# The first tiles of a two-layer convolution kernel: channel 0's Toeplitz tiles read from SBUF, and a reordered start

## The reference

```
h  = sin(freq * (z @ w1 + b1)); h = sin(freq * (h @ w2 + b2)); h = sin(freq * (h @ w3 + b3))
hx = (h @ wo) * decay                       # the same with the Y weights gives hy: [256, 64] each
y  = causal 2-d convolution of x with the outer product hx[:, c] * hy[:, c]     (done by FFT)
x1 = y + x * bias[c]

scores = x1 @ x1.T / 16                     # per image and channel, 256 x 256
x2  = x1 + sum(scores * weights[c], -1, keepdims)
out = (x2 - mean) * rsqrt(var + eps) * gamma[c] + beta[c]    # mean and var per channel
```

## Time and profile before

| | us |
|---|---|
| median of 3 runs | 950.36 (950.07 to 951.35) |
| the profiled execution | 953.63 |
| its span, first to last instruction | 950.9 |
| PE busy | 930.9 (98%) |
| DVE busy | 749.4 (79%) |
| ACT busy | 682.0 (72%) |
| POOL busy | 672.5 (71%) |

### The profile page before, as it was taken

How to read it: one execution, slowest core, us unless ns; L and a number is a source line. 1 busy time by engine, 2 the same in 40 slices (tenths; PEclk the granted TensorE clock), 3 DMA queues, 4 the chain that set the end, 5 groups by cost and what they waited for, 6 DMA issues and landing times.

```text
span 950.9 us, 18901 instructions
## 1 busy us (share of the span) xinstructions
PE 930.9 (98%) x5312; PEld 815.0 (86%) x5312; DVE 749.4 (79%) x2457; ACT 682.0 (72%) x1088; POOL 672.5 (71%) x520
## 2 busy tenths in 40 slices
PE   7999999999999999999999999999999999999994
PEld 5888888888888888888888888888888888888883
DVE  2677887887877888887887887887887878887886
ACT  2447777777677777777777778777777778777776
POOL 2676777776687777777777776776776776776752
PEclk9999999999999999999999999999999999999997
DMA  7767999997899999989798999979799999988954
GB/s 222 265 170 219 251 257 301 261 241 291 228 276 288 208 303 289 272 237 290 199 307 293 213 287 303 267 248 287 228 271 302 246 252 296 274 247 293 256 141 187
DMA packets 91439, 244.09 MB, mean 257 GB/s; under 512 B 17184, under 2 KB 42016, under 8 KB 83232
## 3 DMA queue, kind: packets, MB, share of 16 engines
q1 hardware_dynamic: 73568, 235.73, 85.0%
q10 hardware_dynamic: 17856, 8.20, 3.4%
HBM read 176.52 MB, written 67.37 MB: 256 GB/s over the span
## 4 chain that ended last, share of the span: by engine, by line
PE 78%; POOL 9%; issue 8%; DVE 2%; DMA 1%; ACT 1%; POOLq 0%; DVEq 0%
PE ps_c L525 30%; PE ps_u L525 26%; PE ps_z L525 22%; POOL zl L417 3%; POOL xl L397 3%; POOL toep L390 2%; POOL wl L405 1%; POOL rstd L378 1%; DVE z_sb L718 1%; DMA toep_whole<-filters_padded 1%; DVE ul L758 0%; ACT uh L464 0%; POOL stat L371 0%; DMA par<-params_in 0%; DVE products L731 0%
## 5 line engine op out<-in xcount | busy, mean ns | idle before, releaser
L417 POOL TENSOR_TENSOR zl<-z_sb,zh 128x1024 fp32r<-128x1024 f32 x127 | 304.1, 2395 | 241.1 <-ACT zh L510 241.1
L731 DVE CUSTOM_DVE_ANT_0 products<-z_sb,ps_c 128x256 bf16<-128x256 f32 x504 | 182.2, 418 | 147.7 <-PE ps_c L525 147.7
L485 ACT ACTIVATE out_sb<-z_sb,shift,gain 128x256 f32<-128x256 f32 x496 | 257.3, 591 | 21.1 <-DMA out<-out_sb 15.7
L525 PE MATMUL ps_z<-uh,toep 128*128 128x512 f32 x768 | 271.4, 408 | 0.2 <-DVE z_sb L718 0.2
L464 ACT ACTIVATE uh<-ps_u 128x1024 fp32r<-128x1024 f32 x127 | 130.5, 1028 | 165.9 <-PE ps_u L525 165.9
L525 PE MATMUL ps_u<-toep,xh 128*128 128x256 f32 x1016 | 235.1, 313 | 2.8 <-POOL toep L390 2.4
L525 PE MATMUL ps_c<-zh,wh 128*128 128x512 f32 x504 | 196.3, 390 | 1.3 <-POOL zl L417 1.2
L525 PE MATMUL ps_c<-zh,wl 128*128 128x512 f32 x504 | 196.1, 389 | 0.0
L525 PE MATMUL ps_c<-zl,wh 128*128 128x512 f32 x504 | 196.1, 389 | 0.0
L525 PE MATMUL ps_u<-toep_whole,xt_sb 128*128 128x128 f32 x1016 | 195.8, 274 | 0.0
L742 DVE BATCH_NORM_STATS2 stat<-z_sb 128x6 f32<-128x256 f32 x512 | 179.4, 413 | 0.1
(11 more groups left out here) (79 smaller groups left out, 913.7 us busy)
## 6 DMA issues: line engine op xcount, KB each, us to landing
xt_sb<-xt_in SPq DMA_DIRECT2D x64, 1024.0 KB, 10.8
x_sb<-x_in SPq DMA_DIRECT2D x128, 512.0 KB, 9.1
out<-out_sb SPq DMA_DIRECT2D x124, 512.0 KB, 7.5
w_sb<-wt_in SPq DMA_DIRECT2D x64, 256.0 KB, 7.8
toep_whole<-filters_padded SPq DMA_DIRECT2D x64, 256.0 KB, 7.8
everyone<-partition_moments ACTq DMA_DIRECT2D x62, 128.0 KB, 8.7
out<-z_sb SPq DMA_DIRECT2D x2, 512.0 KB, 3.1
out<-z_sb SPq DMA_DIRECT2D x4, 256.0 KB, 3.4
```

The source lines that it names most:

```text
L417: nc.gpsimd.tensor_tensor(low, z_sb[:, r, h], high.bitcast(F32), ALU.subtract)\
L485: last = nc.scalar.activation(to[:, k, b], z_sb[:, r, h, k, b], ACT.Identity, bias=shift[:, r, g:g + 1], scale=gain[:, r])
L525: return nc.tensor.matmul(o, a, b, start=start, stop=stop)
L731: last = nc.vector.tensor_tensor_reduce(products[:, cs.slot(2), k, b], z_sb[:, r, h, k, b], bank[:, k, b], 1.0 / math.sqrt(SIDE), 0.0, ALU ...
```

## The change

Seven edits, in the order of time:

1. In the filter's layers the argument of half 1 is computed by ACT straight from PSUM (an Identity activation with scale freq / 2 pi and bias `bias_turns`, a new 128 x 3 tile that DVE fills once) and no longer by DVE. DVE's order is now argument 0, turns 0, part 0, turns 1, part 1. The table of the sine is asked for by a dummy activation at the very start. `WARM_LAYER` goes from 3 to 2, `WARM_TOEPLITZ` from 28 to 14.
2. Channel 0's two Toeplitz parts no longer come from DRAM. Each is one DMA of 128 KB from one partition of `filt` in SBUF, 128 overlapping windows of 1 KB: part 1 (Y) first, then the store to DRAM, then part 0 (X). Channel 1 on still come from DRAM.
3. ACT and POOL split channel 0's parts one by one, each with a semaphore of its own for part 1.
4. PE's first product u(0) runs in two passes over its four places: the first without the low part of the tile, and the high times low products behind them, behind a wait for that low part. The first z then waits for part 0.
5. In the first five steps ACT rounds u at the head of the step and not after the x and w parts.
6. Channel 1's tile is split one step earlier, in front of xh of its own step, on ACT and POOL.
7. Statistics take two images at once: bn_stats over 512 numbers in which the two images' numbers alternate (it keeps even and odd numbers apart), so two instead of four per pair, and bn_aggr takes 24 numbers instead of 48.

```diff
-WARM_FIRST, WARM_LAYER, WARM_TOEPLITZ = 3, 3, 28
+WARM_FIRST, WARM_LAYER, WARM_TOEPLITZ = 3, 2, 14
...
+    def toeplitz_step(st):
+        if st.static() and 2 <= st.number() <= 3:
+            return st.trail(0 if st.number() == 2 else LAG_T + 1)
+        return st.trail(LAG_T)
...
+            def load_first_toeplitz(f, landed):
+                row = filt[f * CH:f * CH + 1, 1:1 + SIDE]
+                windows = bass.AP(row.tensor, row.offset, [row.ap[0], [1, P], [1, SIDE]])
+                sp.dma_start(toep_whole[:, 0, f, :], windows).then_inc(landed, 16)
...
             sp.wait_ge(filt_ready, 1)
+            load_first_toeplitz(1, first_s_landed)
             sp.dma_start(pad_dram[:, :, :].rearrange("f c n -> (f c) n"), filt[:, :])\
                 .then_inc(filt_stored, 16)
+            load_first_toeplitz(0, t_landed[0])
             sp.wait_ge(filt_stored, 16)
...
                 ts = st.trail(LAG_LOAD_T)
-                if starts(ts):
+                if starts(ts) and not first_channel(ts):
...
-                means = stat[:, r].rearrange("p g (h s) -> p g h s", h=2)[:, :, :, 1]
-                nc.gpsimd.tensor_tensor(means, means, red[:, r].unsqueeze(2).broadcast_to([P, GROUPS, 2]),
-                                        ALU.add).then_inc(shifted, 1)
+                means = stat[:, r].rearrange("p g (b s) -> p (g b) s", b=PAIR)[:, :, 1]
+                nc.gpsimd.tensor_tensor(means, means, red[:, r], ALU.add).then_inc(shifted, 1)
...
-                ts = st.trail(LAG_T)
-                if starts(ts):
+                def low_toeplitz(ts, parts):
                     t = ts.ring(2)
                     wait_chan(pool, th_ready, ts, 1)
-                    nc.gpsimd.tensor_tensor(toep[:, t, :, 1], toep_whole[:, ts.ring(XR)],
-                                            toep[:, t, :, 0].bitcast(F32), ALU.subtract)\
+                    nc.gpsimd.tensor_tensor(toep[:, t, parts, 1], toep_whole[:, ts.ring(XR), parts],
+                                            toep[:, t, parts, 0].bitcast(F32), ALU.subtract)\
                         .then_inc(tl_ready, 1)
+                ts = toeplitz_step(st)
+                if starts(ts):
+                    if first_channel(ts):
+                        pool.wait_ge(first_sh_ready, 1)
+                        nc.gpsimd.tensor_tensor(toep[:, 0, 1, 1], toep_whole[:, 0, 1],
+                                                toep[:, 0, 1, 0].bitcast(F32), ALU.subtract)\
+                            .then_inc(first_sl_ready, 1)
+                    else:
+                        low_toeplitz(ts, slice(0, 2))
                 if active(st):
...
+                if starts(ts) and first_channel(ts):
+                    low_toeplitz(ts, slice(0, 1))
...
+            act.wait_ge(const_ready, 4)
+            nc.scalar.activation(sine_loaded[:, :], minus_half[:, :], ACT.Sin)
             for layer in range(3):
+                act.wait_ge(layer_done, 2 * layer + 2)
+                if layer == 0:
+                    act.wait_ge(bias_turns_ready, 1)
+                nc.scalar.activation(arg[:, HALVES[1]], ps_u[:, 1, 0, 0:P], ACT.Identity,
+                                     bias=bias_turns[:, layer:layer + 1], scale=freq_turns[:, 0:1])\
+                    .then_inc(second_arg, 1)
                 for i, half in enumerate(HALVES):
-                    act.wait_ge(reduced, 6 * layer + 6 + i)
+                    act.wait_ge(reduced, 5 * layer + 4 + 2 * i)
                     nc.scalar.activation(hid[:, half], part[:, half], ACT.Sin, scale=TWO_PI_BELOW)\
                         .then_inc(hid_ready, 1)
+            def round_u(us):
+                if active(us):
+                    wait(act, u_done, us, 1)
+                    wait(act, y_done, us, -1)
+                    nc.scalar.activation(uh[:, us.slot(2)], u_bank(us)[:, :, :, :], ACT.Copy)\
+                        .then_inc(uh_ready, 1)
             def stage(st):
+                filling = st.static() and st.number() <= 4
+                if filling:
+                    round_u(st.trail(LAG_U))
+                def high_toeplitz(ts):
+                    r = ts.ring(XR)
+                    parts = slice(0, 2)
+                    if first_channel(ts):
+                        parts = slice(0, 1)
+                        act.wait_ge(first_s_landed, 16)
+                        nc.scalar.activation(toep[:, 0, 1, 0], toep_whole[:, 0, 1], ACT.Copy)\
+                            .then_inc(first_sh_ready, 1)
+                    act.wait_ge(t_landed[r], ts.turn(XR) * 16)
+                    wait(act, y_done, ts, -2)
+                    nc.scalar.activation(toep[:, ts.ring(2), parts, 0], toep_whole[:, r, parts], ACT.Copy)\
+                        .then_inc(th_ready, 1)
+                ts = toeplitz_step(st)
+                if starts(ts) and filling and ts.channel() == 1:
+                    high_toeplitz(ts)
...
+                if starts(ts) and not (filling and ts.channel() == 1):
+                    high_toeplitz(ts)
+                if not filling:
+                    round_u(st.trail(LAG_U))
...
+                if first_channel(zs):
+                    pe.wait_ge(tl_ready, 1)
...
                 us = st.trail(LAG_U)
                 if active(us):
                     r, t = us.ring(XR), us.ring(2)
-                    if us.first_of_channel():
+                    first = first_channel(us) and not second_pair(us)
+                    if first:
+                        pe.wait_ge(first_sh_ready, 1)
+                    elif us.first_of_channel():
                         wait_chan(pe, tl_ready, us, 1)
                     wait(pe, xl_ready, us, 1)
                     if not second_pair(us):
                         wait(pe, ul_ready, us, 0)
                     s = us.slot(4)
-                    for h in range(BLOCKS):
-                        rows = slice(P * h, P * (h + 1))
-                        for b in range(PAIR):
-                            o = u_bank(us)[:, h, b, :]
-                            mm(o, xh[:, s, b, rows], toep[:, t, 1, 0, :], True, False)
+                    places = [(h, b, slice(P * h, P * (h + 1))) for h in range(BLOCKS) for b in range(PAIR)]
+                    for h, b, rows in places:
+                        o = u_bank(us)[:, h, b, :]
+                        mm(o, xh[:, s, b, rows], toep[:, t, 1, 0, :], b == 0 or not first, False)
+                        if not first:
                             mm(o, xh[:, s, b, rows], toep[:, t, 1, 1, :], False, False)
-                            mm(o, xl[:, s, b, rows], toep[:, t, 1, 0, :], False, False)
-                            last = mm(o[:, P:SIDE], xt_sb[:, r, PAIR * us.half() + b, 1, rows],
-                                      toep_whole[:, r, 1, 0:P], False, True)
+                        mm(o, xl[:, s, b, rows], toep[:, t, 1, 0, :], False, False)
+                        last = mm(o[:, P:SIDE], xt_sb[:, r, PAIR * us.half() + b, 1, rows],
+                                  toep_whole[:, r, 1, 0:P], False, not first)
+                    if first:
+                        pe.wait_ge(first_sl_ready, 1)
+                        for h, b, rows in places:
+                            last = mm(u_bank(us)[:, h, b, :], xh[:, s, b, rows], toep[:, t, 1, 1, :], False,
+                                      b == PAIR - 1)
...
                                     None, ALU.mult).then_inc(reduced, 1)
+            dve.wait_ge(reduced, 1)
+            nc.vector.tensor_scalar(bias_turns[:, :], par[:, COL_BIAS:COL_BIAS + 3], freq_turns[:, 0:1],
+                                    None, ALU.mult).then_inc(bias_turns_ready, 1)
             for layer in range(3):
+                dve.wait_ge(layer_done, 2 * layer + 1)
+                nc.vector.tensor_scalar(arg[:, HALVES[0]], ps_u[:, 0, 0, 0:P],
+                                        par[:, COL_BIAS + layer:COL_BIAS + layer + 1],
+                                        freq_turns[:, 0:1], ALU.add, ALU.mult).then_inc(reduced, 1)
                 for i, half in enumerate(HALVES):
-                    dve.wait_ge(layer_done, 2 * layer + 1 + i)
-                    dve.wait_ge(reduced, 6 * layer + 1 + i)
-                    nc.vector.tensor_scalar(arg[:, half], ps_u[:, i, 0, 0:P],
-                                            par[:, COL_BIAS + layer:COL_BIAS + layer + 1],
-                                            freq_turns[:, 0:1], ALU.add, ALU.mult).then_inc(reduced, 1)
-                for i, half in enumerate(HALVES):
-                    dve.wait_ge(reduced, 6 * layer + 2 + i)
+                    if i == 0:
+                        dve.wait_ge(reduced, 5 * layer + 2)
+                    else:
+                        dve.wait_ge(second_arg, layer + 1)
                     nc.vector.tensor_scalar(turns[:, half], arg[:, half], ROUND_MAGIC, ROUND_MAGIC,
                                             ALU.add, ALU.subtract).then_inc(reduced, 1)
```

(11 more changed lines are left out.)

21 lines of the change are left out of this document (7 added, 14 removed).

## The result

The changed kernel takes 949.26 us (median of 20 runs, 948.46 to 951.58) against 951.22 (20 runs) for the kernel before, beside which it ran: a ratio of 0.9979, interval 0.9973 to 0.9985, so 2.0 us faster with 1.4 to 2.6 as bounds. The forecast was 6.0 us and 944.4; the 944.4 starts from 950.36, the median of three runs, and from 951.22 it would have been 945.2. The profiled execution took 948.99 us with a span of 947.0.

A forecast was written before the change was run, and what follows sets the result against it. PE, busy 98% of the span, was taken as the bound, so only start and end could gain: 5.7 us at c(0) plus 0.25 made 6.0, from 953.63 to 947.6, or 944.4 for the median; range 942.7 to 949.0.

The forecast's parts named there:

- The filter layers: Start: three layers' argument-to-sine steps shorten, 0.8 us gained (bounds 0 and 1.1), filt ready at 11.2 instead of 11.98.
- Part 1 lands 3.5 us after its issue: Start: channel 0's 128 KB SBUF read takes 3.5 us, bounds 1.9 and 8.7, and lands at 14.7.
- rival A: Start: each one-partition read takes 6 to 7 us; gain only 1.5 to 2 us, time 948.5; chance 15%.
- The store lands at 15.0, just behind part 1: Start: the filter store, queued behind part 1's read, lands at 15.0 instead of 13.86.
- Channel 1's tile, 5.1 us: Start: the tile's load follows the store, takes 5.1 us and lands at 20.15.
- What is late next: Start: channel 1's tile sets u(2), 4.1 us later at 24.25; c(0) follows after 4.8, at 29.05.
- Full clock under u(0): Start: constant products cover nearly all of the wait for part 1, so PE's clock stays at the upper level.
- The tail: End: two bn_stats take 1.3 us against 1.40 for four; with a shorter bn_aggr, 0.2 to 0.3 us less.
- B: Start: part 0, landing at D, delays ACT before uh(0); decides from D = 24.5, at worst 954 us; chance 7%.
- C: Start: the SBUF read lands in 1.9 us, u(2) at 22.85; gain 7.1 + 0.25, time 943.0; chance 15%.
- D: Start: late loads of x(0), xt(2) or x(1) set the pace; gain 0 to 1.9, about 949.5 us; chance 8%.
- E: Loop: DVE becomes the bound if alternating bn_stats costs over 2.3 ns per number; chance 3%.

The follow-up runs named there:

- experiment 1: Changed kernel with each window of channel 0's two SBUF reads taken from the partition it goes to, channel 0's values wrong: 944.67 us, one run.
- experiment 2: Changed kernel with each part read by four DMAs from four partitions, values wrong: 949.38 us for neighbouring partitions, 950.21 for partitions four apart, one run each.
- experiment 4: Changed kernel with both SBUF reads issued on ACT's queue, the store left on SP's: 948.44 us with 14 constant products, 947.53 with 28.
- experiment 3: Changed kernel with 28 constant products instead of 14, nothing else changed: 949.71 us (10 runs), ratio 0.998 to the kernel before.
- experiment 7: Changed kernel with the statistics read in storage order, 256 numbers of one row and then of the other: 950.26 us, one run.
- experiment 5: Changed kernel with channel 0's two parts read from DRAM behind the store: 946.95 us with 14 constant products, 946.13 with 28, 946.34 with 28 run again.
- experiment 6: Changed kernel with channel 0's parts read from DRAM behind a separate first store of its two filter rows, 24 constant products: 946.23 us (6 runs), ratio 0.9947.

## Why the prediction was wrong

- **The filter layers: right.** Argument to sine takes 7.35 - 6.32 = 1.03 us (forecast 1.06, before 1.43), and filt is ready at 11.16 (forecast 11.2). The 0.8 us came in full here; in the profiles of the variants, where these instructions are the same, it is ready between 11.13 and 11.50, and at 11.8 in the two with the slower pace.
- **"Part 1 lands 3.5 us after its issue": this step failed.** It took 6.6. The 85 GB/s of the earlier trace rows was taken for the pace of any small source. It was DRAM's; one SBUF partition gave 28 (experiments 1 and 2). The range for this term, 1.9 to 8.7, held it, and rival A is what happened: part 1 at 17.8 (measured 17.78), the store at 18.2 (18.30), channel 1's tile at 23.3 (24.58), part 0 at 23 (21.33), u(2) at 28 to 28.5 (28.59), a gain of 1.5 to 2 us (1.4 at u(2), 2.0 in the time). Its 15% was too little; its 6 to 7 us for the read hold the measured 6.6. Nothing in the trace of before had a source in one partition, and the value was chosen by bytes and not by where the bytes lie.
- **"The store lands at 15.0, just behind part 1": it followed.** It landed at 18.30, just behind part 1, as the step says. The link was right and its input wrong: behind a read of 2.05 us the store lands in 2.14 (experiment 1), and issued beside the slow read, but done with it first, in 1.86 and 2.08 (experiment 4). Together the two make 3.3 us.
- **Channel 1's tile, 5.1 us: 6.27.** The rest of part 0's read ran beside it until 21.3, but that is not the whole of it: it took 5.9 with fast reads (experiment 1), and 5.8 and 6.1 in experiments 3 and 7 with the same slow ones. Why it takes longer than the first tile did before isn't shown. That is another 1.2 us. 3.3 + 1.2 = 4.5 is the whole lateness of ACT at 24.60 against 20.15, and of c(0) at 33.34 against 29.05 (4.3).
- **What is late next: right.** Channel 1's tile sets u(2), by ACT's four instructions and ul(1), with 4.0 us between (forecast 4.1), and u(2) to c(0) takes 4.75 (forecast 4.8). Experiment 1, with the read faster than assumed (2.05 us), gave c(0) at 28.83.
- **Full clock under u(0): wrong, without a price.** PE idled for 3.56 us and the clock fell, but experiment 3 shows the slack behind it. In experiments 4 and 5, where u(0) is on the path, 28 products bring c(0) 0.5 and 1.6 us forward in the profiles; the times don't show it beyond their intervals.
- **The tail: the right way, and small** (0.33 up to the last norms, 0.64 to the span's end, for 0.25). The two statistics take 1.30 us as forecast, though the terms given for it, 0.14 and 1.05 ns a number, add up to 1.37 for two: one starts before the last has ended (706 ns each, 1.30 for both). The Trainium skill's row that would have made them 1.9 (Vector Engine (DVE) Microarchitecture Reference, section on the SBUF access granule) is for another instruction and a longer hop; here 706 ns for 512 numbers, and 22 ns for the hop, decide against it.
- **Rivals.** B's wait (part 0 in front of uh(0)) appeared at 21.35, 3.2 us before D = 24.5, and cost nothing. C didn't come; even experiment 1, with part 1 in 2.05 us, took 944.67 and not 943.0, since the store landed at 14.13 (13.6 there) and the tile took 5.9. D didn't occur: no engine waited for x or xt in the start, in the changed kernel or in experiment 1. E didn't: 0.706 us an instruction, and DVE's idle time grew. (The chances of B and E add up to 0.10, not 0.09.)

The place chosen to read the gain was the right one. In each of the twelve profiles of the changed kernel and its variants the span has 913.6 to 914.1 us left behind the start of c(0), with the stall in the loop taken off where there is one, while c(0) itself goes from 28.83 to 33.66.

## What to carry to other kernels

Before a DMA's size is divided by a bandwidth, look at how many partitions its source spans: many copies of one SBUF row come at one partition group's pace, and a detour by DRAM can be faster than the direct read. A slow transfer is paid for by everything issued behind it, here on its own queue and on the other one alike, so put the small transfer on which others wait ahead of it. Compute a forecast's chain once with the unknown at each of its bounds, and let the chances follow how little the trace says of it.

## What the runs showed of the hardware that was not expected

**One SBUF partition as source** gives 22 to 28 GB/s to all 16 DMA engines together, which the profile counts as busy for 0.83 of the time; four neighbours give no more, and reading the 128 partitions, with the store beside it, gave 285.

**A second queue is no way around it.** From ACT's queue part 1 took 6.75 us as well, and it held up SP's queue: for 3 us that queue moved nothing, with a load of 256 KB issued on it, and the load landed after 8.7 us, 0.5 behind the second slow read. Only the store, whose issue was done 0.2 us before the read's, got through in 2.1.

**PE's pace at full granted clock.** In two of the profiles, the first one of experiment 5 with 28 and that of experiment 6, the constant products ran slower at the same granted clock of 1.00. The same stretch in the first run of the version of experiment 5 with 28:

```profile
13.00:14.00 1.00, 1.00 (x4) 0.81 (x3) 0.00 (x0) 0.00 (x0) 0.00 (x0) 1.00 0.23 83
```

and in its repeat:

```profile
13.00:14.00 1.00, 1.00 (x6) 0.84 (x5) 0.00 (x0) 0.00 (x0) 0.00 (x0) 1.00 0.01 3
```

Four instructions in a microsecond and not six; the 28 took 9.14 us and not 6.66, filt was 0.67 late already, and c(0) started at 33.20 and not 30.07. That execution took 948.87 us, and of the 12 runs of this version 4 lie at 947.6 to 949.6 and 8 at 945.7 to 946.4, which fits two such paces, but the stall in the loop (up to 1.2 us) could lift a run as well, and only two of the 12 were profiled. In experiment 6 the 24 took 8.17 us. What sets the pace stays open. In a single run the gain of this version is anything from 2 to 5.8 us.
